# One unit more of score look-ahead in an attention stage, with the row maxima turned and sent earlier

## What is computed

```python
qkv = x @ Wqkv + bqkv                  # x after layer norm
qkv_a = xa @ Wqkv_aux + bqkv_aux       # xa is the context
dots = einsum('bhqd,bhkd->bhqk', q, k) * scale        # 16 heads of 8
dots_aux = einsum('bhqd,bhkd->bhqk', q, ka) * scale
p, pa = softmax(dots), softmax(dots_aux)
out = (p @ v) * (1.0 - gate) + (pa @ va) * gate
x = x + tanh(g_xattn) * (out @ Wo + bo)
x = x + tanh(g_ffn) * (sum over 8 of 64 experts, chosen per token, + one shared expert)
```

## Time and profile before

| | |
|---|---|
| time, median of 3 runs | 871.06 us (869.92 to 871.6) |
| the profiled execution | 874.03 us, span 872.2 us |
| PE (TensorE matmul) busy | 832.4 us, 95% |
| DVE (VectorE) | 690.8 us, 79% |
| POOL (GpSimd) | 637.7 us, 73% |
| ACT (ScalarE) | 565.8 us, 65% |
| granted TensorE clock | 1.000 |

### The profile page before, as it was taken

The page is one execution under the profiler, slowest core; times in us unless marked ns, Lnnn a source line. Parts: engine busy times, 40 slices in busy tenths (PEclk is TensorE's granted clock), DMA queues, the critical chain, the costliest instruction groups (busy, mean ns, idle before and its releaser), DMA issues.

```text
span 872.2 us, 20170 instructions
## 1 busy us (share of the span) xinstructions
PE 832.4 (95%) x6733; PEld 646.8 (74%) x6733; DVE 690.8 (79%) x1656; ACT 565.8 (65%) x964; POOL 637.7 (73%) x602
## 2 busy tenths in 40 slices
PE   5899999998898889999999999999999999999997
PEld 3467777776675668888888888887888888888885
DVE  6789899998888858778777877967976977877655
ACT  4377888887777756566566567548557556656554
POOL 2476888887883357887787786887787788778785
PEclk9999999999999999999999999999999999999999
DMA  5567777777653156646554654654746555655552
GB/s 131 175 173 188 182 192 189 186 193 182 168 156 81 32 138 151 151 119 148 134 134 123 168 133 109 169 129 110 179 119 143 145 134 126 148 131 140 143 137 58
DMA packets 113747, 125.27 MB, mean 144 GB/s; under 512 B 28000, under 2 KB 76064, under 8 KB 112208
## 3 DMA queue, kind: packets, MB, share of 16 engines
q1 hardware_dynamic: 110768, 123.47, 56.8%
q10 hardware_dynamic: 2880, 0.59, 0.4%
HBM read 103.55 MB, written 19.96 MB: 142 GB/s over the span
## 4 chain that ended last, share of the span: by engine, by line
PE 75%; DMA 6%; DVE 2%; issue 2%; ACT 2%; POOL 1%; SPq 0%; DVEq 0%; ACTq 0%; POOLq 0%
PE bank L1963 20%; PE bank L1965 20%; PE bank L1964 20%; PE bank L1305 4%; DMA stack_q<-nmaxT 3%; PE bank L1292 3%; PE bank L1279 2%; DMA stack_k<-k_scratch 1%; PE bank L1261 1%; PE bank L1249 1%; DMA cwb<-wts_scratch 1%; ACT prob L787 1%; PE bank L1313 1%; PE bank L1940 1%; PE bank L1326 1%
## 5 line engine op out<-in xcount | busy, mean ns | idle before, releaser
L1640 POOL TENSOR_TENSOR hid<-act,cwb 128x512 f32<-128x512 f32 x264 | 424.4, 1616 | 125.7 <-DVE act L1867 71.7
L1693 ACT ACTIVATE silu<-bank 128x512 f32<-128x512 f32 x256 | 152.8, 597 | 193.7 <-PE bank L1965 189.2
L1867 DVE TENSOR_TENSOR act<-silu,bank 128x512 f32<-128x512 f32 (+1 forms) x264 | 180.5, 684 | 118.8 <-ACT silu L1693 76.6
L1963 PE MATMUL bank<-xhi,weights_hi 128*128 128x512 f32 x520 | 206.7, 397 | 0.4 <-ACT silu L1693 0.4
L1875 DVE TENSOR_TENSOR hlo<-hid,hhi 128x512 fp32r<-128x512 f32 x256 | 199.4, 779 | 7.3 <-ACT hhi L1699 7.0
L1965 PE MATMUL bank<-xlo,weights_hi 128*128 128x512 f32 x520 | 204.1, 392 | 0.0
L1964 PE MATMUL bank<-xhi,weights_lo 128*128 128x512 f32 x520 | 203.8, 392 | 0.0
L984 DVE TENSOR_REDUCE mx<-bank 128x4 f32<-128x512 f32 x256 | 167.5, 686 | 22.4 <-PE bank L1279 18.7
L1699 ACT ACTIVATE hhi<-hid 128x512 fp32r<-128x512 f32 (+1 forms) x264 | 165.0, 625 | 13.3 <-POOL hid L1640 10.9
L787 ACT ACTIVATE prob<-bank 128x1024 f32<-128x1024 f32 x128 | 131.0, 1024 | 64.0 <-PE bank L1292 61.8
L1965 PEld LDWEIGHTS bank<-xlo,weights_hi 128*128 128x128 f32 x520 | 97.6, 188 | 22.0
(11 more groups left out here) (235 smaller groups left out, 1003.0 us busy)
## 6 DMA issues: line engine op xcount, KB each, us to landing
cwb<-wts_scratch SPq DMA_DIRECT2D x174, 384.0 KB, 5.4
stack_k<-k_scratch SPq DMA_DIRECT2D x30, 384.0 KB
k_scratch<-parts_k SPq DMA_DIRECT2D x15, 384.0 KB, 3.3
stack_q<-q_scratch SPq DMA_DIRECT2D x30, 192.0 KB
k_scratch<-parts_k SPq DMA_DIRECT2D x15, 256.0 KB, 3.9
q_scratch<-parts_q SPq DMA_DIRECT2D x15, 192.0 KB, 2.2
xin<-in_x_dram SPq DMA_DIRECT2D x16, 128.0 KB, 2.5
cin<-in_ctx_dram SPq DMA_DIRECT2D x16, 128.0 KB, 2.6
```

The costliest lines, as they stand in the source:

```text
L1640: pool.tensor_tensor(h_buf[k][:], a_buf[k][:], cwb[slot][:, q % GP, :], ALU.mult).then_inc(h_ok, 1)
L1693: act.activation(s_buf[k % RS][:], g_bank[k % 2][:], ACT.Silu).then_inc(s_ok, 1)
L1867: nc.vector.tensor_tensor(a_buf[k % RS][at], s_buf[k % RS][at], u_bank[k % 3][at], ALU.mult).then_inc(a_ok, 1)
L1963: nc.tensor.matmul(bank, w[0], mh, start=first, stop=False)
```

## The change

Eight units of scores are computed ahead in place of seven. So in each round of b both units are those of batch b + 2 (the 8th unit of b + 1 used to come in round one of b), the last maximum of b + 2 is taken at the end of b, and `minus_max(b + 2)` is issued there, in round four. `turn_max(b + 1)` moves ahead of the projections of round one. `evac_nmax(b + 1)` moves from after the second maximum of round one to after the first. `shift_rows(b + 1)` moves from after the second round's exponentials to the first round, behind `copy_o` (L801, the copy of the weighted sums). Late batches keep the old places of the turn, the copy and the DMA. No instruction is added or left out.

```diff
-AHEAD = 7
@@ ScalarE
+                late = last or (before_last and k == BODY - 1)
                 for r in range(ROUNDS):
                     exps(b, r)
-                    if r == 1 and not (last and k == BODY - 1):
-                        shift_rows(b + 1)
                     if r == 0 and not first:
                         copy_o(b - 1, 1 - odd)
+                    if r == (1 if late else 0) and not (last and k == BODY - 1):
+                        shift_rows(b + 1)
@@ VectorE
-        for u in range(AHEAD):
+        for u in range(UNITS):
             maxima(1, 1, u)
             if u == 4:
                 copy_ka(2)
+        minus_max(1, 1, 3)
...
                 for u in range(UNITS):
-                    if u + AHEAD < UNITS:
-                        if one_more:
-                            maxima(b + 1, 1 - odd, u + AHEAD)
-                    elif two_more:
-                        maxima(b + 2, odd, u + AHEAD - UNITS)
-                    if u == UNITS - AHEAD - 1 and one_more:
-                        if b == NB - 2:
-                            dve.wait_ge(fe_ok, 1)
-                        minus_max(b + 1, 1 - odd, min(n + 3 + odd, NC))
-                    if u == 1 and one_more:
+                    if u == 0 and b == NB - 2:
+                        dve.wait_ge(fe_ok, 1)
+                        minus_max(NB - 1, 1, NC)
+                    if two_more:
+                        maxima(b + 2, odd, u)
+                    if u == (1 if late else 0) and one_more:
                         evac_nmax(b + 1)
+                    if u == 7 and two_more and b + 2 < NB - 1:
+                        minus_max(b + 2, odd, min(n + 4, NC))
@@ TensorE
-        for u in range(AHEAD):
+        for u in range(UNITS):
             scores(1, u, 0)
             scores(1, u, 1)
...
-                        if u + AHEAD < UNITS:
-                            ahead = (b + 1, u + AHEAD) if one_more else None
-                        else:
-                            ahead = (b + 2, u + AHEAD - UNITS) if two_more else None
+                        ahead = (b + 2, u) if two_more else None
...
+                    if r == 0 and one_more and not late:
+                        wait(pe, nm_ev, b + 1)
+                        turn_max(b + 1)
                     if r == 0 and odd and n + 3 < NC:
                         wait(pe, v_ev, n + 2)
                         project_qk(n + 3, 1 - i)
...
-                    if r == 0 and one_more and not late:
-                        wait(pe, nm_ev, b + 1)
-                        turn_max(b + 1)
```

More of the change, by code:

```diff
@@ L1193, in body @@
                 one_more, two_more = not (last and k == BODY - 1), not (last and k >= BODY - 2)
+                late = last or (left == 1 and k == BODY - 1)
                 for u in range(UNITS):
-                    if u + AHEAD < UNITS:
-                        if one_more:
-                            maxima(b + 1, 1 - odd, u + AHEAD)
-                    elif two_more:
-                        maxima(b + 2, odd, u + AHEAD - UNITS)
-                    if u == UNITS - AHEAD - 1 and one_more:
-                        if b == NB - 2:
-                            dve.wait_ge(fe_ok, 1)
-                        minus_max(b + 1, 1 - odd, min(n + 3 + odd, NC))
-                    if u == 1 and one_more:
+                    if u == 0 and b == NB - 2:
[4 more added lines that the diff above has]
+                    if u == (1 if late else 0) and one_more:
                         evac_nmax(b + 1)
+                    if u == 7 and two_more and b + 2 < NB - 1:
+                        minus_max(b + 2, odd, min(n + 4, NC))
                     if u == 1 and first:
```

## The result

The change takes 880.66 us, median of 4 runs (878.79 to 881.86); the kernel before took 871.33 (869.92 to 873.84) beside it. The ratio is 1.0092, 95% interval 1.0065 to 1.0118: slower by 0.9%, and 6.5 us above the upper end of the predicted range, 874.2. (The two medians alone are 9.3 us, 1.1%, apart.) The profiled execution took 878.79 us, span 876.0 us, 3.8 us above the span before. That difference is smaller than that of the medians because this execution is the fastest of its four, and the profiled one of before, 874.03 us, stood above its median.

A forecast was written before the change was run, and what follows sets the result against it. Bounds: TensorE's own work, with the keys' stack chain just above it. Shift waits −5.1, stack waits −2.3 + 7.0 gave −0.4, with late batches −0.7 us: 870.4 us against the median of 871.06, range 866.6 to 874.2.

The forecast's parts named there:

- The rest: Remaining effects: later residual harmless, turn and projection swapping at 0, late batches −0.3 us, last two batches 0.
- the nine waits listed: Stepped TensorE waits for the keys' stack in even batches 6 to 18, 20 and 24, summed as 7.0 us.
- rival C: Stack's second half late for round two's fourth unit, stalling even batches; +3.3 us at 0.5 us late, 874.4; chance 0.15.
- Shift DMA earlier: Shift DMA issued about 1.8 us into the batch, 1.16 earlier; TensorE's waits through batch 24 go, −5.1 us.
- The DMA in ScalarE's queue: In odd batches the DMA holds ScalarE ahead of high_of, lengthening the keys' stack chain by 0.36 us, to 24.8.
- Rival B: Toll on the keys' stack chain not paid, as ScalarE's queue runs on or GpSimd's backlog governs; 868.9 us, chance 0.37.
- Rival D: Round two's exponentials on ScalarE slip behind the DMA; at 0.3 us slip +2.9 us, 874.0; chance 0.09.
- The toll of 7.0 us of waits for the stack: TensorE's waits for the keys' stack in even batches grow from 2.3 to 7.0 us.
- Stack needed earlier: Even batches read the first half 0.24 us sooner, the second 2 us sooner; bounds 0 and 1.8 per batch, taken 0.
- Turn ahead of the projections: In round one on TensorE, turn and projection swap places with the same gaps: 0.

The follow-up runs named there:

- e1: The change with heads scored ahead rotated to 8, 10, 12, 14, 0, 2, 4, 6 and the second-half stack wait at the fifth unit: 873.21 us, ratio 1.0015.
- e2: The kernel before with only the head order changed, so rounds two and four each get one unit sharing rows with the shifted scores: 883.36 us, ratio 1.0151.
- e8: e1 with heads reordered so both units ahead in rounds two and four share rows with the shifted scores: 895.40 us, ratio 1.0250.
- e0: The kernel before, unchanged, run once more for a second profile: 871.22 us.
- e3: The change with the shift DMA put back behind the second round's exponentials: 886.29 us, ratio 1.0160.
- e9: e1 with turn, copy of the turned maxima and shift DMA all at their old places, leaving eight units ahead alone: 877.66 us, ratio 1.0040.
- e10: e5 with TensorE's wait for GpSimd's clear of the shift rows taken two units earlier: 873.91 us, ratio 1.0004.
- e7: e1 with heads in natural order, so all eight units ahead share rows with the shifted scores: 1137.34 us, ratio 1.3036.
- e12: The kernel before with only GpSimd's clearing of the shift rows moved ahead of its second rest_of: 874.33 us, ratio 1.0020.
- e4: e1 with the turn of the maxima put back behind round one's projections, its copy left early: 889.75 us, ratio 1.0198.
- e5: e1 with ScalarE's high_of put ahead of the shift DMA in round one: 873.37 us, ratio 1.0006.
- e11: e10 with GpSimd's clearing of the shift rows moved ahead of its second rest_of: 868.99 us, ratio 0.9958.

## Why the prediction was wrong

- **The step that failed is "The rest", with its steady lengths.** It put the change in the rounds at nothing ("The turn and the projection swap places with the same gaps: 0"), and the sum stepped through batches of 8.00 and 7.86 us. They became 8.46 and 8.27. Of the 11.3 us in batches 1 to 26, 26 × 0.39 = 10.1 are two units that share their rows (e1, e2, e8), 26 × 0.08 = 2.1 the first round, and 13 × 0.07 = 0.9 came back in round three. No rival named it. (Of its sums, the nine waits listed add up to 7.15 us where it has 7.0, and its range ends at 874.2 where rival C comes to 874.4; neither matters here.) The diff swaps which unit meets which round, and the heads of a unit decide the rows; the earlier trace rows already read `64*128` and `52*128`, the two halves side by side. The Trainium skill (TensorE: Matmul & The Clock Gate, "Part 3: Packing small matmuls — row/col tiling") has the rule: weight loads run beside matmuls in flight only where the row groups differ. The trace agrees: one sharing unit costs 0.19 to 0.20 us. The prediction did not weigh it.
- **Shift DMA earlier: right.** "About 1.8 us" was 1.78; every wait for it ahead of batch 27 is gone, and `minus_max` in round four did no harm. Its worth was sized from one execution, where e0 has only 0.7 us of such waits. By pairs it is 5.6 us within the change (e3), and 4.5 us between the medians of e1 and e9, which were not measured together (by their ratios 2.2 us, and those intervals overlap).
- **The DMA in ScalarE's queue: right**, +0.34 where 0.36 was put, down to the last split (15.14 against 14.80). Rival B's ground falls. Rival D did not occur in the change: the exponentials of round two start 3.22 us in, but 0.25 of it is waiting for TensorE's longer round.
- **The toll of 7.0 us of waits for the stack: not paid in the change** (1.7 us in batches 1 to 26), as batches longer by 0.43 us give the chain 25.2 us in place of 23.9. With short rounds (e1) more of it shows: 5.2 us. e1 is level with the kernel before and 2.8 us above the predicted 870.4: the prediction priced the change as if its heads had been rotated. How far that agreement is luck is open, as two profiles of the kernel before differ by 5.8 us in the waits for the shift DMA and by 1.7 us in those for the stack.
- **Stack needed earlier: half right.** The second half was in time (rival C did not occur). But the first scores of unit 0 as the second matmul cost the odd batches from 5 on 0.1 us, in a wait already satisfied (e10), and the even ones about as much.
- **Turn ahead of the projections:** put at 0, it gains 0.04 us a batch together with the earlier copy and DMA (e9 against e1).

Open: what costs the even batches the same 0.1 us (the wait for the stack itself would have to move, which was not tried), why a wait for the stack is nothing in one batch and 3 us in another, and whether shared rows or something else held the half pace so long in e8 and e7.

## What to carry to other kernels

Where two streams of small matmuls are interleaved, a change of look-ahead is a change of partners: write down for each round which rows of TensorE both use, before and after, ahead of pricing anything else. Where two chains are just above the engine's own work, shortening one may show nothing; here neither the early shift rows (e1) nor the shorter stack chain (e12) beat the kernel before, and both together, with `high_of` first and one wait instruction moved, gave 0.4%. An engine's copy that is put ahead of its other work must have its producer moved too, or it holds the queue (e4: 16 us).

## What the runs showed of the hardware

A long wait of TensorE could be paid twice. In e10 TensorE stood 2.30 us for the stack at 87.7 to 90.1 us in batch 6; then (columns as above):

```profile
88.00:90.00 2.00, 0.00 (x0) 0.00 (x0) 0.49 (x3) 0.33 (x1) 1.84 (x4) 1.00 0.83 191
90.00:92.00 2.00, 1.92 (x31) 1.58 (x32) 1.18 (x3) 1.25 (x2) 1.84 (x4) 0.78 0.92 236
92.00:94.00 2.00, 2.00 (x19) 1.76 (x17) 0.46 (x2) 0.68 (x2) 1.76 (x4) 0.50 0.38 105
```

The granted clock fell to 0.50 with TensorE busy again, and rounds one and two took 5.54 and 2.28 us: besides the wait of 2.30 us, some 0.9 + 0.5 us. In e0 (a wait of 1.7 us) some 1.5 us were lost in the same way.

Other waits of the attention stage were followed by such a fall too: 2.6 us in e1, 3.0 in e5, 2.2 and 1.5 in e9, 2.2 and 1.4 in e3, 1.8 in e12. Others were not: 1.7 in the profiled execution of before, 1.7 in e11, 1.6 and 1.5 in e3, 1.5 in e2. So one late landing cost 0.6 (e10) and 0.9 (e0) of its own length again, and the length of the wait alone does not say whether it will. Nor does the granted clock tell all: e8 ran its batch 1 at half pace while it read 1.00 (e8 above).
